# Hybrid block: ScalarE's attention steps without a loop, state sums as column tiles, negated maxima on GpSimd

## The reference

```python
# attention a: 16 query heads, 4 key/value heads, head size 16, all 2048 keys
scores = jnp.einsum('bghnd,bhsd->bghns', q, k)
attn = jax.nn.softmax(scores / SCALE, axis=-1)
out = jnp.einsum('bghns,bhsd->bghnd', attn, v)
...
# attention b: linear, causal, no softmax
energy = jnp.einsum('bhnd,bhmd->bhnm', q, k) * mask      # lower triangle
out = jnp.einsum('bhnm,bhmd->bhnd', energy, v)
```

## Time and profile before

| | |
|---|---|
| median of 3 runs | 2127.48 us (2120.81 to 2131.93) |
| profiled execution, its own time | 2126.95 us |
| its span, first to last instruction | 2125.1 us |
| busy PE / DVE / ACT / POOL | 95% / 86% / 70% / 9% |
| mean granted TensorE clock | 0.968 of full speed |
| exponentials run (start of the first, of the last) | 122.7 us to 1450.3 us |
| state sums run | 1668.8 us to 1939.4 us |

### The profile page before, as it was taken

One profiled execution on the slowest core, in us unless ns is written; L12 is line 12 of the kernel. 1 busy time (PEld: TensorE's weight loads), 2 busy tenths in 40 slices (PEclk: granted clock), 3 DMA queues, 4 the chain that ended last, 5 costly groups with the idle time before them and its releaser, 6 DMA issues.

```text
span 2125.1 us, 47800 instructions
## 1 busy us (share of the span) xinstructions
PE 2012.0 (95%) x13990; PEld 819.9 (39%) x13990; DVE 1817.2 (86%) x3396; ACT 1488.2 (70%) x2939; POOL 181.6 (9%) x298
## 2 busy tenths in 40 slices
PE   7899999999999999999999999989897799998995
PEld 4323333333333333333333333334432466665432
DVE  7899999999999999999999999944459877777348
ACT  5358888888888888888888888854367544445657
POOL 2300000000000000000000000311006211112001
PEclk9879999999999999999999999999998899998997
DMA  5432212211221221121121122131000000000002
GB/s 156 123 96 60 69 43 55 69 46 46 68 56 42 65 63 42 52 73 45 45 72 53 43 66 61 33 121 54 1 1 1 1 1 1 1 0 1 1 1 80
DMA packets 110232, 101.34 MB, mean 48 GB/s; under 512 B 52240, under 2 KB 91424, under 8 KB 110096
## 3 DMA queue, kind: packets, MB, share of 16 engines
q1 hardware_dynamic: 110096, 99.92, 17.2%
HBM read 78.79 MB, written 20.77 MB: 47 GB/s over the span
## 4 chain that ended last, share of the span: by engine, by line
PE 83%; DVE 7%; ACT 4%; issue 4%; DMA 1%; SPq 0%; ACTq 0%; DVEq 0%; POOL 0%; POOLq 0%
PE ps L700 22%; PE ps L675 15%; PE ps L723 10%; PE ps L729 10%; PE ps L836 6%; PE ps L845 3%; PE ps L939 2%; PE ps L948 2%; ACT YT L1115 2%; PE ps L987 2%; PE ps L689 1%; PE ps L968 1%; PE ps L1018 1%; PE ps L641 1%; DVE X L1609 1%
## 5 line engine op out<-in xcount | busy, mean ns | idle before, releaser
L1489 DVE TENSOR_REDUCE mx<-ps 128x1 f32<-128x512 f32 x2048 | 1278.6, 682 | 28.3 <-PE ps L675 22.9
L1115 ACT ACTIVATE YT<-ps 128x512 f32<-128x512 f32 x2048 | 1058.0, 606 | 277.2 <-PE ps L729 251.3
L700 PE MATMUL ps<-YT,work 128*32 128x512 f32 x4096 | 546.2, 605 | 0.0
L675 PE MATMUL ps<-work 64*128 64x512 bf16 x2048 | 461.2, 389 | 8.3 <-DVE mx L1489 6.1
L723 PE MATMUL ps<-work 64*128 64x512 bf16 x2048 | 406.0, 378 | 6.6 <-ACT YT L1115 3.4
L729 PE MATMUL ps<-work 34*128 34x512 bf16 x2048 | 400.5, 378 | 0.0
L675 PEld LDWEIGHTS ps<-work 64*128 64x128 bf16 x2048 | 144.5, 93 | 612.5 <-DVE mx L1489 540.7
L723 PEld LDWEIGHTS ps<-work 64*128 64x128 bf16 x2048 | 161.9, 94 | 116.2 <-ACT YT L1115 42.1
L700 PEld LDWEIGHTS ps<-YT,work 128*32 128x32 f32 x4096 | 80.7, 108 | 123.0 <-issue 87.6
L1829 POOL COPY work<-vals 128x512 f32 (+1 forms) x32 | 19.6, 613 | 1223.0 <-PE ps L700 1222.9
L729 PEld LDWEIGHTS ps<-work 34*128 34x128 bf16 x2048 | 101.0, 94 | 49.3 <-issue 1.6
(11 more groups left out here) (179 smaller groups left out, 1803.6 us busy)
## 6 DMA issues: line engine op xcount, KB each, us to landing
work<-k_scr SPq DMA_DIRECT2D x640, 64.0 KB, 2.2
work<-q_scr SPq DMA_DIRECT2D x640, 32.0 KB, 1.8
o_scr<-o_sb SPq DMA_DIRECT2D x32, 256.0 KB, 2.1
X<-in_L_attn_a_x_dram SPq DMA_DIRECT2D x8, 512.0 KB, 7.4
work<-negt SPq DMA_DIRECT2D x256, 1.0 KB
work<-o_scr SPq DMA_DIRECT2D x16, 256.0 KB
work<-inv_scr SPq DMA_DIRECT2D x16, 256.0 KB
out_dram<-X SPq DMA_DIRECT2D x8, 512.0 KB, 2.9
```

The costliest lines, as they stand in the source:

```text
L675: mm(ps[:, bank_of[x], :], qa[rows, p, jp, qt * P:(qt + 1) * P], ka[rows, p, kc_ * CH:(kc_ + 1) * CH], start=True, stop=True).then_inc(a_m ...
L700: m = mm(ps[32 * j:32 * j + 32, 7, :], vst[:, p, t, :], prob(GROUP * t + j), start=t == 0, stop=t == KTILES - 1)
L1115: fn(prob(u), ps[:, S_BANK + u % S_RING, :], ACT.Exp, scale=HD ** -0.5).then_inc(exp_ok, 1)
L1489: dve.tensor_reduce(mx[:, p, at_:at_ + 1], ps[:, bank_of[x], :], AX_X, ALU.max).then_inc(a_max, 1)
```

## The change

Three edits. ScalarE's 30 steps from the third on are written out by Python's `for`; the instructions of a step are the same, without the register arithmetic. VectorE's two small operations for the high and low parts go; GpSimd makes them in three (high part, minus the maximum in fp32, their difference), and VectorE's transpose stands after reduction x = 4 where it was after x = 3. The state sums become eight products of 128x32 weights by 32 columns, each giving one 32x32 block (two heads), where two products gave 128x128; VectorE's product with diag becomes two, which read the 32 columns of a half four times over.

```diff
--- before.py
+++ after.py
@@ -187,6 +187,7 @@
         o_sb = sb("o_sb", [P, 2, CH])
         mx = sb("mx", [P, 2, MAXU])
         mxq = sb("mxq", [P, GROUP * QT])
+        mxn = sb("mxn", [P, GROUP * QT])
         negq = sb("negq", [P, NEG], BF16)
         negt = sb("negt", [P, NEG], BF16)
         gmc = sb("gmc", [P, KT, NCH])
@@ -272,6 +273,11 @@
 
             pairs = v_x[:, p, kt * HPK:(kt + 1) * HPK].rearrange("p (i a) d -> p i (a d)", a=2)
             return bass.AP(pairs.tensor, pairs.offset, [pairs.ap[0], pairs.ap[1], [32 + HD, 2], [1, HD]])
+
+        def v_pair(p, kt, i):
+
+            pair = v_x[:, p, kt * HPK + 2 * i:kt * HPK + 2 * i + 2].rearrange("p a d -> p (a d)")
+            return bass.AP(pair.tensor, pair.offset, [pair.ap[0], [32 + HD, 2], [1, HD]])
 
         names = """id_ld w0_ld w_ld consts cols c_dve c_tw n_bn n_mv n_ve n_rs n_sm n_sh n_sp n_xn n_t n_y n_bo
             p_mm p_act p_res p_mid p_low p_val v_ones kb_ones a_mm a_max
@@ -988,8 +994,10 @@
                                    e_m[:, i, 2 * kt + a, :], start=False, stop=a == 1, skip_group_check=True)
                 m.then_inc(l_o, 1)
                 for kt in range(KT):
-                    m = mm(ps[:, 2, kt * P:(kt + 1) * P], qk_r[:, p, DIM + kt * P:DIM + (kt + 1) * P],
-                           v_heads(p, kt), start=first and kt == 0, stop=kt == KT - 1, skip_group_check=True)
+                    for i in range(4):
+                        own = DIM + kt * P + 32 * i
+                        m = mm(ps[32 * i:32 * i + 32, 2, 32 * kt:32 * kt + 32], qk_r[:, p, own:own + 32],
+                               v_pair(p, kt, i), start=first and kt == 0, stop=kt == KT - 1, skip_group_check=True)
                 m.then_inc(l_s, 1)
 
             def rows(n):
@@ -1118,9 +1126,7 @@
 
             step(0, 0, before=False)
             step(0, 1)
-            step(1, 0)
-            step(1, 1)
-            with act.Fori(2, STEPS // 2) as i:
+            for i in range(1, STEPS // 2):
                 step(i, 0)
                 step(i, 1)
             collect(STEPS - 1, STEPS // 2 - 1, 1)
@@ -1463,19 +1469,8 @@
 
             def row_maxima(s, p):
                 dve.wait_ge(a_max, REDUCED * (s + 1) - 1)
+                wait(dve, nm_low, s)
                 dve.tensor_reduce(mxq[:], mx[:, p].rearrange("p (a b) -> p a b", b=KC), AX_X, ALU.max).then_inc(a_max, 1)
-
-            def negated_high(s, last=False):
-                dve.wait_ge(a_max, REDUCED * (s + 1) + (0 if last else 1))
-                wait(dve, nm_t, s)
-                dve.tensor_scalar(negq[:].rearrange("p (g r a) -> p g r a", g=2, r=2)[:, :, 0, :],
-                                  mxq[:].rearrange("p (g a) -> p g a", g=2), -1.0, None, ALU.mult).then_inc(nm_hi, 1)
-
-            def negated_low(s):
-                dve.wait_ge(nm_hi, s + 1)
-                parts = negq[:].rearrange("p (g r a) -> p g r a", g=2, r=2)
-                dve.scalar_tensor_tensor(out=parts[:, :, 1, :], in0=mxq[:].rearrange("p (g a) -> p g a", g=2), scalar=-1.0,
-                                         in1=parts[:, :, 0, :], op0=ALU.mult, op1=ALU.subtract).then_inc(nm_low, 1)
 
             def negated_turn(s):
                 dve.wait_ge(nm_low, s + 1)
@@ -1492,11 +1487,7 @@
                     if before:
                         if x == 0:
                             row_maxima(s - 1, 1 - p)
-                        if x == 1:
-                            negated_high(s - 1)
-                        if x == 2:
-                            negated_low(s - 1)
-                        if x == 3:
+                        if x == 4:
                             negated_turn(s - 1)
 
             maxima(0, 0, before=False)
@@ -1507,8 +1498,6 @@
                 maxima(2 * i, 0)
                 maxima(2 * i + 1, 1)
             row_maxima(STEPS - 1, 1)
-            negated_high(STEPS - 1, last=True)
-            negated_low(STEPS - 1)
             negated_turn(STEPS - 1)
             constants()
 
@@ -1698,8 +1687,11 @@
                 if reset:
                     dve.memset(s_x, 0.0).then_inc(l_sx, 1)
                 else:
-                    dve.tensor_tensor(s_x.rearrange("p k n -> p (k n)"), ps[:, 2, 0:DIM],
-                                      diag[:].rearrange("p h d -> p (h d)"), ALU.mult).then_inc(l_sx, 1)
+                    for kt in range(KT):
+                        sums = ps[:, 2, 32 * kt:32 * kt + 32].rearrange("p (g n) -> p g n", g=1).broadcast_to((P, 4, 32))
+                        m = dve.tensor_tensor(s_x[:, kt, :].rearrange("p (g n) -> p g n", g=4), sums,
+                                              diag[:, kt * HPK:(kt + 1) * HPK].rearrange("p (g a) d -> p g (a d)", a=2), ALU.mult)
+                    m.then_inc(l_sx, 1)
 
             def gated(n, p):
 
@@ -1829,6 +1821,19 @@
                 pool.tensor_copy(vst[:, p].rearrange("p t d -> p (t d)"),
                                  vals[:, kv_of(s)].rearrange("p t d -> p (t d)")).then_inc(v_st, 1)
 
+            def negated_parts(s, last=False):
+
+                parts = negq[:].rearrange("p (g r a) -> p g r a", g=2, r=2)
+                pool.wait_ge(a_max, REDUCED * (s + 1) + (0 if last else 1))
+                wait(pool, nm_t, s)
+                minus = minus4[:, 0:1].broadcast_to((P, GROUP * QT))
+                pool.tensor_tensor(parts[:, :, 0, :], mxq[:].rearrange("p (g a) -> p g a", g=2),
+                                   minus.rearrange("p (g a) -> p g a", g=2), ALU.mult).then_inc(nm_hi, 1)
+                pool.tensor_tensor(mxn[:], mxq[:], minus, ALU.mult).then_inc(nm_hi, 1)
+                pool.wait_ge(nm_hi, 2 * (s + 1))
+                pool.tensor_tensor(parts[:, :, 1, :], mxn[:].rearrange("p (g a) -> p g a", g=2), parts[:, :, 0, :],
+                                   ALU.subtract).then_inc(nm_low, 1)
+
             pool.wait_ge(p_val, CPG)
             values(0, 0)
             values(1, 1)
@@ -1836,9 +1841,13 @@
                 residue(c)
                 low(c)
             pool.wait_ge(p_val, NCH)
+            negated_parts(0)
             with pool.Fori(1, STEPS // 2) as i:
+                negated_parts(2 * i - 1)
                 values(2 * i, 0)
+                negated_parts(2 * i)
                 values(2 * i + 1, 1)
+            negated_parts(STEPS - 1, last=True)
 
 
             pool.wait_ge(w_ld, 16 * len(weights))
```

## The result

The changed kernel takes 2090.15 us in the median (2089.54 to 2090.99, 4 runs); the kernel before, on the same chip, 2126.77 (2120.81 to 2131.93). The ratio is 0.9829, interval 0.9803 to 0.9855: faster by 1.7%. The forecast was 2109.3 us, range 2101 to 2121. The direction was right, the size half of what came, and the time lies outside the range. The profiled execution takes 2089.54 us, its span is 2087.7 us, 37.4 us shorter than before's where 17.7 were forecast.

The account below looks back on a forecast made before the run. VectorE was taken to bound the softmax attention, TensorE the linear attention. Terms -17.0 - 3.5 + 0.5 + 0.5 + 1.8 = -17.7 us took 2126.95 us to 2109.3 us, range 2101 to 2121 us.

Parts of the forecast that it names:

- What bounded the kernel: VectorE sets the pace in softmax attention, missing 17.0 us at ScalarE's 13 round ends; TensorE does in linear attention.
- ScalarE without the loop: Softmax attention: writing out ScalarE's steps removes 13 round ends, -17.0 us.
- written-out code costs nothing: ScalarE in softmax attention: fetching the written-out code taken as 0, bounds 0 and 17.0 us.
- High and low parts: Softmax attention: two small operations leave VectorE, 0.11 us a step, -3.5 us in 31 steps.
- The waits that come in: VectorE's transpose now waits for GpSimd's chain of 0.95 us with hand-overs; no stall taken in the steps.
- Spare time: Between the end of GpSimd's chain and VectorE's transpose, 1.4 us to spare in each step.
- The loads land in time: Loads behind the transpose, needed at a step's start: 0.4 us to spare remain, cost taken as 0.
- The +0.5 us ahead of the first step: Before the first attention step no exponentials run, so the transpose's delay goes through: +0.5 us.
- the +0.5 of the forecast: After the last reduction the transpose comes later behind GpSimd's chain, delaying the first output projection: +0.5 us.
- The state sums: Linear tiles: small products take 0.51 us at L987's rate; with the uncovered load +0.06 us a tile, +1.8 us.
- the full load behind column tiles: Linear tiles: the uncovered full weight load, 0.19 us, moves on to L1018, neither saved nor doubled.
- the lower bound for the state sums: Linear tiles: if time went with the columns streamed, -0.32 us a tile, -10 us in about 30 tiles.

Follow-up runs that it names:

- e1_loop: Changed kernel with only ScalarE's loop of 14 rounds of two steps put back: 2117.09 us, ratio to the kernel before 0.9954.
- e9_unroll_only: Kernel before with one edit alone, ScalarE's attention steps written out: 2108.54 us, ratio 0.9917.
- e5_loop4: Changed kernel with ScalarE's steps from the fifth on in a loop of 7 rounds of four steps: 2095.46 us.
- e3_parts_dve: Changed kernel with high and low parts made by VectorE again and the transpose after reduction x = 3: 2096.91 us.
- e7_pool_late: Changed kernel with twelve more small products in GpSimd's chain ahead of VectorE's transpose: 2112.25 us.
- e8_value_tiles: Changed kernel with the first stage's value projections as four 128x32 column tiles each: 2090.13 us.
- e6_twice: Changed kernel with each of the eight state products issued twice, so the sums come out doubled: 2099.04 us.

## Why the forecast was wrong

**What bounded the kernel: right.** ScalarE's gaps at the 13 round ends and the 26 waits of VectorE behind them come and go together with the loop: e1_loop and e9_unroll_only show it.

**ScalarE without the loop: right, size -17.0 forecast, -18.1 measured** (e9_unroll_only; put back on top of the other two edits, in e1_loop, the loop costs 24.8 us between the first and the last fold). That written-out code costs nothing held: one packet each 62.5 us, no gap. The price of an end is not a property of the loop alone, though (2.0 us in before, 2.5 in e1_loop, 1.3 in e5_loop4).

**High and low parts: right, size -3.5 forecast, -4.8 measured.** The two reductions of the earlier trace rows start 1.36 us apart over the two operations, and the prediction took off 2 x 0.624 us, the mean over 41 reductions. That mean mixes two kinds: three of four reductions start 0.60 us after the one before, and every fourth 0.68 us after it. The two in question are of the short kind: after has them without the operations, at 555.62, 556.22 and 556.81, 1.20 us apart. 1.36 - 1.20 = 0.16 us, which is the 0.155 us of e3_parts_dve.

**The waits that come in: right.** Spare time 1.4 forecast, 1.55 measured; e7_pool_late shows the wall behind it. The loads land in time; no row puts a wait on them. The +0.5 us ahead of the first step did not come: the transpose is at 115.30 where it was at 114.81, but the first exponential starts at 122.6 as before. Behind the last reduction the transpose starts 0.35 us later than before, and the first output projection 0.96 us later (23.42 us behind the start of that reduction, 22.46 before), about twice the +0.5 of the forecast; yet the whole stretch to the linear attention is only 0.1 us longer.

**The state sums: this step failed.** The prediction took "the value from L987, the nearest in weights' shape": 0.51 us for the state sums where 0.12 came, so +1.8 us were forecast for the tiles and -9.7 measured. That is 11.5 of the 19.7 us by which the forecast missed. The mistake is in reading 1.01/32 as the time of a record. The records of after lie in groups of four, one for each quarter of the array's columns. Within a group they start 0.007 us apart, and the next group starts 0.109 us later with 128 columns, 0.03 us later with 32. Before's own records show the same groups for L987, 0.109 us apart. With 64 columns, in e8_value_tiles, the groups start 0.056 us apart. So in these runs a group of four is one pass, whose time goes with its columns (0.030, 0.056 and 0.109 us for 32, 64 and 128); the price of one record is a quarter of a pass with 128 columns, and cutting the columns to a quarter cuts the pass to about a quarter. The weight loads lie beside one another and ahead of the products. This is one line and its durations in after, min/median/max in ns, which show how far the records overlap:

```profile
L999 PEld LDWEIGHTS ps<-work x16: 110/112/113, 1708.3 to 1708.5; 128*32 128x32 f32 x16
L999 PE MATMUL ps<-work x16: 192/196/196, 1708.5 to 1708.6; 128*32 128x32 f32 x16
```

Sixteen loads of 112 ns each within 0.3 us, and sixteen products of 196 ns that all start in 0.11 us. The Trainium skill (TensorE: Matmul & The Clock Gate, Part 3: Packing small matmuls) gives the span of packed tiles as the duration of one product and about 4 ns for each further tile. The trace agrees on the form of it within a group of four, with 7 ns between the records for its 4. The prediction had weighed the full load behind column tiles instead, and that part held: its price moved from the state sums (0.64 - 0.45 = 0.19 us) to the output projection (1.06 - 0.86 = 0.20 us), neither saved nor doubled.

**What had no term: the clock in the tail.** The last feed-forward is the same code, yet 5.1 us shorter. By the granted clock TensorE ran at half its speed (1.2 of 2.4 GHz) for 42.3 us of it before and 32.2 after; half of the difference is 5.05 us. The profiles differ in this among themselves: e1_loop has 191.7 us of tail with 45.8 at half clock, e5_loop4 188.2 with 35.6, e9_unroll_only 187.4 with 31.4, e6_twice 187.0 with 29.0. The tail is longer where the half-clock time is longer, though not in a fixed proportion (before and e1_loop have the same tail with 42.3 and 45.8 us); 191.7 came with both kernels that have ScalarE's round of two steps, and no other. That the clock makes the difference is argued from its size; no run holds the clock fixed. A later start alone doesn't do it: e7_pool_late enters the tail at 1923.2 us, near e1_loop's 1926.7, and takes 188.2. What sets the windows of half clock wasn't found.

Had I taken the lower bound for the state sums, the sum would have been 2097.5 us; the remaining 7 us are the tail and small terms. The range ended at 2101 because the bound was held for unlikely, on the strength of a rate that had been worked out wrongly.

## What to carry to other kernels

A mean over records that run side by side is not the price of one: look at the starts of single records before you scale it by shape. For the fp32 column tiles of these runs the time went by the columns streamed, four records at once, so a product of which only the diagonal blocks are wanted is cheaper cut to them, as long as TensorE sets the pace of that stretch (it did in the linear tiles; in the first stage waits for tokens and for a load took the gain). A hardware loop whose body has to be fetched again left 1.3 to 2.6 us of idleness at each round end here, which a short body or written-out code avoided; measure it where it stands, since size of the body and price don't go in proportion. And take off the mean time of a long row of instructions only where the ones in question are of the mean kind.

## What the runs showed that I had not expected

- ScalarE's round end leaves a gap of 2.0 to 2.6 us with two steps in a round, 1.3 with four, and nothing that can be seen with eight exponentials. VectorE's own loop over the steps shows no such gap in before.
- The same loop is worth 19 us in before (e9_unroll_only) and 27 us in after (e1_loop).
- Runs of one kernel spread with the clock: among nine of before the fastest, 2120.2 us, had a mean granted clock of 0.973 and the slowest, 2131.7, one of 0.968; the three in between at 0.968 take 2126.2 to 2128.7 us, so the mean clock tells only part of it. The kernels with the two-step round spread widest (e1_loop 9.0 us in 12 runs, before 12.7 in 17), the others 1.5 to 7.5 us in 4 to 6 runs each; whether that is the number of runs alone stays open.
- GpSimd's small operations take 0.22 us each beside VectorE's reductions, and start 0.18 and 0.30 us apart in the step shown, where the same form of operation took 1.17 us beside products of two inputs.
